# Attention stage: one-head loops, P times V in query halves, paired transposes and projections, diagonal blocks copied by GpSimd

## Time and profile before

| | us |
|---|---|
| median of 3 runs | 3308.22 (3308.05 to 3309.66) |
| the profiled execution | 3313.78 |
| its span, first to last instruction | 3312.2 |
| PE busy | 3196.9 (97%) |
| DVE busy | 2544.1 (77%) |
| ACT busy | 2007.7 (61%) |
| POOL busy | 1454.5 (44%) |

### The profile page before, as it was taken

The page is one execution under the profiler, slowest core; times in us unless marked ns, Lnnn a source line. Parts: engine busy times, 40 slices in busy tenths (PEclk is TensorE's granted clock), DMA queues, the critical chain, the costliest instruction groups (busy, mean ns, idle before and its releaser), DMA issues.

```text
span 3312.2 us, 54697 instructions
## 1 busy us (share of the span) xinstructions
PE 3196.9 (97%) x14467; PEld 1714.4 (52%) x14468; DVE 2544.1 (77%) x2917; ACT 2007.7 (61%) x3525; POOL 1454.5 (44%) x1795
## 2 busy tenths in 40 slices
PE   7799999998999999999999999999999999999998
PEld 3355444555555555555555555555555555555554
DVE  7612444234998989898988999898999899889995
ACT  4312320334676767676766777777777777777775
POOL 4677770013244444444444445544444444444443
PEclk9899999999999999999999999999999999999999
DMA  7613886665998989898988899999999999899997
GB/s 299 266 68 117 309 267 153 223 228 187 236 236 216 231 214 229 212 231 219 229 218 218 216 233 243 261 231 226 231 230 230 229 230 228 219 225 232 227 227 183
DMA packets 342733, 737.33 MB, mean 223 GB/s; under 512 B 129517, under 2 KB 177400, under 8 KB 342160
## 3 DMA queue, kind: packets, MB, share of 16 engines
q1 hardware_dynamic: 311056, 670.55, 76.9%
q0 software_dynamic: 31488, 64.51, 7.0%
HBM read 198.37 MB, written 159.51 MB: 108 GB/s over the span
## 4 chain that ended last, share of the span: by engine, by line
PE 70%; DVE 2%; issue 1%; SPq 1%; ACT 1%; DMA 0%; ACTq 0%; POOL 0%; DVEq 0%; POOLq 0%
PE at_ps L1043 27%; PE at_ps L1073 26%; PE at_ps L1056 9%; PE at_ps L1088 9%; DVE at_half_max L1164 1%; DVE at_blocks L1180 1%; SPq L914 1%; ACT at_prob L1124 0%; DMA at_v<-v_rows 0%; DMA at_moved<-at_blocks 0%; ACT at_scaled L1136 0%; DVE at_neg_max L1169 0%; ACT ahead_xe L1152 0%; SPq L905 0%; POOL at_acc L1003 0%
## 5 line engine op out<-in xcount | busy, mean ns | idle before, releaser
L1164 DVE TENSOR_REDUCE at_half_max<-at_ps 128x1 f32<-128x1024 f32 x1024 | 1206.6, 1219 | 250.9 <-PE at_ps L1043 249.0
L1124 ACT ACTIVATE at_prob<-at_ps,at_neg_max 128x1024 f32<-128x1024 f32 x1024 | 1145.3, 1118 | 333.7 <-DVE at_neg_max L1169 318.3
L1180 DVE STREAM_TRANSPOSE at_blocks<-at_prob 128x1536 f32<-128x1536 f32 x512 | 906.0, 1770 | 1.2 <-ACT at_prob L1124 1.2
L1043 PE MATMUL at_ps<-ahead_k_hl,ahead_q_hh 128*128 128x512 f32 x2048 | 854.4, 417 | 17.7 <-ACT at_prob L1124 10.8
L1003 POOL TENSOR_TENSOR at_acc<-at_acc,at_scaled 128x256 f32<-128x256 f32 x512 | 372.0, 727 | 1064.0 <-ACT at_scaled L1136 1064.0
L1043 PE MATMUL at_ps<-ahead_k_hl,ahead_q_ll 128*128 128x512 f32 x2048 | 810.2, 396 | 0.0
L1073 PE MATMUL at_ps<-at_moved,at_v 128*64 128x512 f32 x3072 | 726.8, 594 | 5.6 <-DMA at_moved<-at_blocks 4.3
L1136 ACT ACTIVATE at_scaled<-at_ps,at_inv 128x256 f32<-128x256 f32 x512 | 242.3, 473 | 354.1 <-PE at_ps L1088 340.0
L1056 PEld LDWEIGHTS at_ps<-keep_ident,at_prob 128*128 128x128 f32 x2048 | 216.1, 141 | 437.9 <-issue 425.5
L1043 PEld LDWEIGHTS at_ps<-ahead_k_hl,ahead_q_hh 128*128 128x128 f32 x2048 | 389.4, 190 | 88.2 <-ACT at_prob L1124 15.5
L1043 PEld LDWEIGHTS at_ps<-ahead_k_hl,ahead_q_ll 128*128 128x128 f32 x2048 | 390.4, 191 | 67.7
(11 more groups left out here) (112 smaller groups left out, 2596.1 us busy)
## 6 DMA issues: line engine op xcount, KB each, us to landing
at_moved<-at_blocks SPq DMA_DIRECT2D x2048, 192.0 KB
ahead_k_hl<-k_parts SPq DMA_DIRECT2D x64, 512.0 KB, 8.0
ahead_q_hh<-q_parts SPq DMA_DIRECT2D x128, 256.0 KB, 5.6
ahead_q_ll<-q_parts SPq DMA_DIRECT2D x128, 256.0 KB, 6.4
xbuf<-pr_zeros SPq DMA_DIRECT2D x32, 512.0 KB, 5.1
q_parts<-pr_part_hi SPq DMA_DIRECT2D x64, 256.0 KB
q_parts<-pr_part_lo SPq DMA_DIRECT2D x64, 256.0 KB
k_parts<-pr_part_hi SPq DMA_DIRECT2D x64, 256.0 KB, 2.2
```

What stands on the lines that cost most here:

```text
L1043: last = nc.tensor.matmul(ps[:, bank, :], q[:, g % 2, j * P:(j + 1) * P], k_hl[:, side, c * CH:(c + 1) * CH], start=first, stop=not first)
L1124: nc.scalar.activation(prob[:, i % 2, half * 1024:(half + 1) * 1024], ps[:, banks[0]:banks[1], :].rearrange("p b c -> p (b c)"), ACT.Exp, ...
L1164: nc.vector.tensor_reduce(half_max[:, i % 2, half:half + 1], ps[:, banks[0]:banks[1], :], AX.XY, ALU.max).then_inc(max_step, 1)
L1180: nc.vector.transpose(blocks[:, parity, :, j, :, :].rearrange("p c t k -> p t c k"), prob[:, (s["s"] - 1) % 2, 0:MOVED * P].rearrange("p ( ...
```

## The change

- The loop over heads has a body of one head. K is loaded twice per head, once for the first eight slots (side 0) and once for the last eight (side 1); W_O likewise.
- DVE turns 13 key tiles of 16, PE three. PE's transposes come in even slots, for the two tiles before, behind the scores, into banks of the early scores; one ACT copy takes both tiles out.
- P times V is done for each key tile in two query halves of 256 columns, so the two array halves hold two halves of the queries. The projection then contracts over 64 rows and gives all 128 queries of a tile; two tiles are projected in each odd slot, side by side on two halves of the rows.
- Of the 16 blocks of the exchange SP moves 12; the four on the diagonal, which stay on their partitions, are copied by POOL, two in each even slot (`diagonal`). P times V waits for `diag_done`.
- POOL gathers two rows in each of the even slots 0 to 6, and waits for them at the beginning of slots 2 to 8; scales and adds two in each of slots 8 to 14; and adds two scaled tiles in each odd slot.

```diff
-MOVED = 12
+MOVED = 13
 TURNED = NS - MOVED
 PV_LAG = 2 * GT
 OUT_LAG = 3 * GT + 1
-LAST = OUT_LAG + TILES
-PV_PLACES = ((12, 16), (0, 4), (4, 8), (8, 12))
+LAST = OUT_LAG + TILES - 1
+GQ = GT // 2
+PV_PLACES = ((13, 16), (0, 5), (5, 9), (9, 13))
 ACROSS = (0, 2, 1, 3)
 EARLY = ((0, 2), (4, 6))
 LATE = (2, 4)
-PV_BANK, TURN_BANK = 6, 7
+PV_BANK = 6
...
                     body(b, 0, s)
-                with eng.Fori(0, H // 2 - 1) as i:
-                    for u in (1, 2):
-                        for s in slots(b, (i, u)):
-                            body(b, (i, u), s)
+                with eng.Fori(1, H - 1) as h:
+                    for s in slots(b, h):
...
+            def next_k(b, h, side):
+                head = b * H + h
+                wait_apart(sp, late_scored, (head - 1) * TILES + (side + 1) * TILES // 2, sp_waits)
+                load_k(sp, scr, start, b, h, side)
...
             def load_wo(b, h, side):
-                wait_apart(sp, projected, (b * H + h - 1) * TILES + 1, sp_waits)
+                wait_apart(sp, projected, (b * H + h) * TILES - TILES // 2 * (1 - side), sp_waits)
...
-                for turn in range(QD):
+                for turn in range(1, QD):
                     for r, c in zip(ACROSS, ACROSS[turn:] + ACROSS[:turn]):
                         sp.dma_start(moved[c * 32:(c + 1) * 32, g % 2, r, :, :, :],
                                      blocks[r * 32:(r + 1) * 32, g % 2, c, :, :, :]
...
+            def head_loads(b, h, before, following):
                 next_q(b, h, 1)
+                next_k(b, h, 1)
                 if before is not None:
                     exchange(*before, GROUPS - 1)
                 next_q(b, h, 2)
                 load_v(b, h, 0)
                 exchange(b, h, 0)
-                load_wo(b, h, side)
+                load_wo(b, h, 0)
                 for place in range(1, GT):
                     load_v(b, h, place)
                 next_q(b, h, 3)
                 if following is not None:
-                    next_k(*following, 1 - side, 0)
+                    next_k(*following, 0)
                 exchange(b, h, 1)
                 if following is not None:
                     next_q(*following, 0)
-                    next_k(*following, 1 - side, 1)
                 exchange(b, h, 2)
+                load_wo(b, h, 1)
...
-                if k % (K // 2) == 0:
-                    wait_apart(pool, gathered[part], n * 64 + 64, pool_waits)
...
+                for k in (s["s"] % K, s["s"] % K + 1):
+                    if s["s"] < K:
+                        nc.gpsimd.indirect_dma_start(
+                            out=row(k), out_offset=None, in_=scr["ye"][:, :],
+                            in_offset=bass.IndirectOffsetOnAxis(ap=g_index[:, k:k + 1], axis=0),
+                            bounds_check=SLOTS, oob_is_err=True).then_inc(gathered[k // (K // 2)], 16)
+                    else:
+                        nc.gpsimd.tensor_scalar(row(k), row(k), g_gain[:, k:k + 1], None, ALU.mult
+                                                ).then_inc(g_scaled, 1)
+                        wait_apart(pool, g_scaled, n * K + k + 1, pool_waits)
+                        nc.gpsimd.tensor_tensor(into, into, row(k), ALU.add).then_inc(g_added, 1)
+                        wait_apart(pool, g_added, n * K + k + 1, pool_waits)
...
+            def diagonal(group, parity, r):
+
+                wait_apart(pool, blocks_done, GT * (group + 1), pool_waits)
+                wait_apart(pool, pv_done, GT * (group - 1), pool_waits)
+                for q in (r, r + 1):
+                    nc.gpsimd.tensor_copy(moved[q * 32:(q + 1) * 32, parity, q, :, :, :],
+                                          blocks[q * 32:(q + 1) * 32, parity, q, :, :, :]).then_inc(diag_done, 1)
+                    wait_apart(pool, diag_done, QD * group + q + 1, pool_waits)
...
+                if i % 2 == 0 and 0 < i <= K:
+                    part = (i - 1) // (K // 2)
+                    wait_apart(pool, gathered[part], s["head"] * 64 + 16 * (i - part * (K // 2)), pool_waits)
+                if s["diag"]:
+                    diagonal(*s["diag"])
...
             def score(s, half):
...
                     if j == 0:
                         pe.wait_ge(q_loaded[g % 2], 32 * (head * 2 + g // 2) + 32)
-                    if i == 0:
-                        pe.wait_ge(k_loaded[side], 32 * s["pair"] + 32)
+                    if i % (TILES // 2) == 0:
+                        pe.wait_ge(k_loaded[side], 16 * head + 16)
                     wait_pos(pe, early_exp, tile - 1)
+                    if i % 2:
+                        wait_pos(pe, copied, s["taken_all"])
+                    else:
+                        wait_pos(pe, scaled, s["projected"])
                     banks, done = EARLY[i % 2], early_scored
                 else:
                     wait_pos(pe, late_exp, tile)
...
             def transpose(s):
-                tile = s["tile"] - 2
-                pe.wait_ge(late_exp, tile + 1)
-                wait_pos(pe, copied, tile)
-                if s["out"]:
-                    wait_pos(pe, scaled, s["out"][0] * GT + s["out"][2])
-                for j in range(TURNED):
-                    t = MOVED + j
-                    last = nc.tensor.transpose(ps[:, TURN_BANK, j * P:(j + 1) * P],
-                                               prob[:, s["s"] % 2, t * P:(t + 1) * P], keep["ident"][:, :])
+
+                pe.wait_ge(late_exp, s["tile"])
+                pe.wait_ge(early_exp, s["tile"])
+                for a in range(2):
+                    for j in range(TURNED):
+                        t = MOVED + j
+                        last = nc.tensor.transpose(ps[:, EARLY[1][0] + a, j * P:(j + 1) * P],
+                                                   prob[:, a, t * P:(t + 1) * P], keep["ident"][:, :])
                 last.then_inc(turned, 1)
...
-                    pe.wait_ge(copied, GT * (group + 1))
+                    pe.wait_ge(copied, GT // 2 * (group + 1))
                     wait_pos(pe, oT_done, group)
                 else:
...
                 pe.wait_ge(v_loaded[place], 16 * (s["head"] + (1 if s["s"] >= PV_LAG else 0)))
                 for t in tiles:
-                    side = t % 2 * DH
-                    p_T = moved[:, parity, :, :, t, :] if t < MOVED else turned_sb[:, parity, t - MOVED, :, :, :]
-                    last = nc.tensor.matmul(ps[side:side + DH, PV_BANK, :], v[:, t, :], p_T,
-                                            start=(place == 0 and t < tiles[0] + 2),
-                                            stop=(place == GT - 1 and t >= tiles[-1] - 1))
+                    for half in range(2):
+                        side, queries = half * DH, slice(half * GQ, (half + 1) * GQ)
+                        p_T = (moved[:, parity, :, queries, t, :] if t < MOVED else
+                               turned_sb[:, parity, t - MOVED, :, queries, :])
+                        last = nc.tensor.matmul(ps[side:side + DH, PV_BANK, 0:GQ * P], v[:, t, :], p_T,
+                                                start=(place == 0 and t == tiles[0]),
...
             def project(s):
-                group, g, j, behind = s["out"]
...
-                for side in (0, DH):
-                    last = nc.tensor.matmul(ps[side:side + DH, TURN_BANK, 0:D],
-                                            oT[:, g % 2, j * P + side:j * P + side + DH], wo[:, s["out_side"], :],
-                                            start=True, stop=True)
-                last.then_inc(projected, 1)
+
+                for n, g, j, half, behind in s["out"]:
+                    if j == 0:
+                        pe.wait_ge(oT_done, s["pv_group"])
+                        pe.wait_ge(wo_loaded[g // 2], 16 * (s["head"] + (0 if behind else 1)))
+                    if half == 0:
+                        pe.wait_ge(early_exp, min(s["s"], TILES) + s["head"] * TILES)
+                        wait_pos(pe, scaled, n)
+                    rows, queries = slice(half * DH, (half + 1) * DH), slice(j % GQ * P, (j % GQ + 1) * P)
+                    nc.tensor.matmul(out_of(s, half), oT[rows, g % 2, queries], wo[rows, g // 2, :],
+                                     start=True, stop=True).then_inc(projected, 1)
...
             def body(b, h, s):
-                if s["late"]:
-                    transpose(s)
                 if s["scores"]:
                     score(s, 0)
                     score(s, 1)
-                if s["out"]:
-                    project(s)
+                project(s)
+                if s["taken"]:
+                    transpose(s)
                 if s["pv"]:
                     times_v(s)
...
             def take(s):
-                group, parity, j = s["turn"]
-                act.wait_ge(turned, s["tile"])
+                group, parity, j = s["taken"]
+                act.wait_ge(turned, s["taken_all"])
```

(56 more changed lines are left out.)

113 lines of the change are left out of this document (36 added, 77 removed).

## The result

The changed kernel takes 3646.07 us (median of 4 runs, 3632.79 to 3653.02) against 3308.14 us for the kernel before (4 runs, 3306.54 to 3309.66) beside it: a ratio of 1.1017, 95% interval 1.0983 to 1.105. The prediction said 3730, in a range of 3400 to 3900.

A forecast was written before the change was run, and what follows sets the result against it. GpSimd's ordered list was to become the period: 90.8 us a head against 77.3, 13.6 more for 31 heads, +422 on 3313.8 gives 3736, less the 5.6 by which the runs' median is lower: 3730 us; range 3400 to 3900.

The forecast's parts named there:

- Copy, 1.7 us: GpSimd's diagonal copies, 16 a head of 1664 elements per partition: 0.18 + 1.54 = 1.7 us each, bounds 0.41 and 4.8.
- Rivals 2 and 3: GpSimd's diagonal copies: cheap at 0.41 us, about 3110 us, chance 0.12; or far dearer at 4.8, about 5270, chance 0.04.
- Landing, 5.8 us: GpSimd's wait, in a head's first half, for two gathers to land before the next copies: 5.8 us per even-odd pair.
- Rival 1: Gathers land early in a head's first half: pairs of 9.4 us, head 80.4, about 3405 us; chance 0.13.
- Second half, 10.4 a pair: GpSimd's list per even-odd slot pair late in a head: copies 4.0, routed rows 4.14, additions 2.26, together 10.4 us.
- The sum: GpSimd's list per head: 4 x 12.0 + 4 x 10.4 + 1.2 = 90.8 us; 13.6 more for 31 heads, +422.
- The low end of the range: 3400 us for the whole kernel, said to be GpSimd copies of 1.6 us with gather landings of 3 us.
- PE, 4.3 to 4.4 us a slot: PE's attention work after the change: two slots cost 8.6 us plus up to 0.2, or 4.3 to 4.4 a slot.
- rival 2: Cheap GpSimd copies leave PE and VectorE as bound, winning 6.2 us on 32 heads: -198, about 3110 us; chance 0.12.
- VectorE, 4.4: VectorE's attention slot: 4.17 + 0.15 for the longer block transpose, plus sum and reciprocal, bringing 4.4 us.
- Jumps back: Loop jumps, 26 for 12: 0.7 us each where PE is the bound, nothing where PE waits anyway.
- Rival 4: Copies between 0.8 and 0.95 us, or GpSimd and PE gains meeting: within 7 us of 3308; chance 0.03.

The follow-up runs named there:

- e4: The change with each of GpSimd's 16 diagonal copies a head cut to 128 of 1664 elements per partition; ratio 0.9716 to the kernel before, 74.3 us a head.
- e5: The change with each of GpSimd's diagonal copies moving half its elements, 832 of 1664 per partition; ratio 0.9959 to the kernel before, 76.8 us a head.
- e7: The change with a group's four copies in slot 4g+6, gathers in fours after slots 2 and 6, awaited in 6 and 10; ratio 0.9995 to the kernel before.
- e1: The change with gathers in fours in slots 0 and 4, awaited in 4 and 8, and four copies together in slot 4g+8; ratio 1.0326 to the kernel before.
- e6: The change with SP moving groups 3 and 0's diagonal blocks, GpSimd copying only groups 1 and 2, gathers awaited in slots 8 and 10; 3240.21 us, ratio 0.9788.

## Why the prediction was right, and where its sizes were off

**The mechanism** was the one forecast. GpSimd's ordered list is the period; the landing stands behind copies that PE waits for. "GpSimd at 75% busy" was too high (62% of the span, 67% of the head above); the idle before its copies is put down to the gathers, PE is at 89% (75 to 80 forecast) with stops, VectorE is idle 14.7 us in the head above (20 forecast), DMA share is 0.74 (under 0.8 forecast). PE's 75 to 80% meant 70.4 us of work in 90.8; it was some 73.9 a head in e4 at a granted clock of 1.00, and 78.4 in the 87.6 of the head above at 0.94, which the forecast left out.

**Copy, 1.7 us**: measured 1.566, 8% less. Lengths of 128, 832 and 1664 took 286, 872 and 1566 ns: 0.83 ns per element plus 0.18 us. The rate of 0.93 taken from copies of 8 and 256 on 128 partitions was a little high, and the fixed part held. Rivals 2 and 3 fall with this. 16 copies x 0.13 = 2.1 us of the 2.8 by which the head was predicted too long.

**Landing, 5.8 us** from the second gather's issue: all gathers of the change landed in 2.8 to 11.5, median 5.8.

```profile
DMA to landing us min/median/max: 2.8/5.8/11.5
```

In the head above the first half's pairs took 11.8 on average where 12.0 (and 1.2 more for the index and jump) was said; less 3.7 for the copies, 2.2 for the gathers and 0.2 for the index that leaves about 5.7. Rival 1 fails with it: only the fastest gathers land in 3 us. The Trainium skill's fit ("DMA: Bandwidth & Descriptors", section "Anatomy of one DMA — SWDGE (gpsimd) path") would by estimate have had them all there in 2.3, and none was.

**Second half, 10.4 a pair**: 10.1.

**The sum**: head 90.8 predicted, 88.0 measured. Times 31 heads, +422 was said and some +335 came: 2.8 x 31 = 87 us, of which three quarters are the copy's rate. The term of the sum that was mis-sized is the copy, and with it nothing else of weight. The low end of the range was mis-summed: copies of 1.6 us with landings of 3 give 4 x 9.2 + 4 x 10.2 + 1.2 = 79 a head by the prediction's own terms, about 3360 us and not 3400.

**PE, 4.3 to 4.4 us a slot**: wrong, and hidden by GpSimd. With the copies shortened a slot is 4.63 to 4.64. Half of the four slots of e4 against my terms: transposes 0.69 (0.88 said), projection 0.67 (0.58), scores 4.13 (3.70), P times V 3.76 (3.44). That reads as if the scores had got slower, and they did not: the chain gives the overlap at a boundary to the piece before or behind. What counts is the time from the first start of a piece to the first start of the next, on PE's timeline, before and in e4:

```profile
2602.70 1.89 PE L1073 MATMUL at_ps<-at_moved,at_v 128*64 128x512 f32 x8
2604.52 0.66 PE L1056 MATMUL at_ps<-keep_ident,at_prob 128*128 128x128 f32 x4
```

```profile
2415.20 1.95 PE L1102 MATMUL at_ps<-at_moved,at_v 128*64 128x256 f32 x16
2417.08 0.50 PE L1070 MATMUL at_ps<-ahead_k_hl,ahead_q_hh 128*128 128x512 f32 x1
```

| per two slots, start to start | before us | e4 us | gain | gain said |
|---|---|---|---|---|
| transposes | 0.83 (8) | 0.76 (6) | 0.07 | 0.30 |
| projection | 0.96 | 0.63 | 0.33 | 0.58 |
| scores | 4.04 | 4.14 (0.04 of it a stop) | -0.10 | 0 |
| P times V | 3.64 | 3.76 | -0.12 | 0 |

I had cut pieces out of the earlier trace rows as if each were its own time; a piece taken away gives back less than its row says. P times V with twice as many products of half the width costs little more: 16 products of 256 columns take 1.88 us, 8 of 512 take 1.82. Had GpSimd not been in the way, "-198" would have been about -93 us, and rival 2 off by half.

**VectorE, 4.4**: its transposes of 1664 took 1.90 us (1.92 said); in e4 it is busy 769 of 800 us beside PE's 796. It was not shown to be a bound.

**Jumps back**: in e4 most heads, each with its jump, take 74.1 to 74.3 us in both batches, and four times the four slots above are 74.3; nothing is left for the jump (0.7 said).

**Rival 4's "everything cancels"** wanted copies of 0.8 to 0.95 us and a time within 7 us of the kernel before. e5 had 0.87 and came out 12 us below it: nearly so. e7 reached it with full copies, by another order of the same work. That was the step no case had: the sum was taken as given by the amounts, while 347 of the 439 us above e4's stage lay in where, and how often, the list waited. Taking the wait for the gathers away while copies stay behind them was not tried, because both then work on the same partitions without an order; what the landings alone cost is therefore shown only by moving them (e1, e7, e6).

## What to carry to other kernels

An engine that waits for each of its own operations has no slack of its own: cost its list as a sum, and put a wait for a transfer as far behind the issue, and as far ahead of what others need, as the list allows; that was worth 9% here with the same copies, gathers and additions. When a load can go to an engine or to the queues, share it by time: the queues while the engine waits for something, the engine while the queues are full. A piece of a chain of waits is not what its removal gives back; measure from the start of one piece to the start of the next.

## What the runs showed of the hardware

- GpSimd copies 32 partitions at 0.83 ns per element plus 0.18 us (286, 872, 1566 ns for 128, 832, 1664), hardly faster than 128 (256 elements on 128 partitions took 412 ns, where this line gives 392), and two in a row on different partitions take the sum, 3.19 us.
- PE's clock followed its stops: 0.91 in the half of a head with waits, 0.98 in the other, where 1 is 2.4 GHz. The product group behind a stop of 3.71 us ran at half its rate, 20 products in 4.54 us:

```profile
2413.43 4.54 PE L1098 MATMUL at_ps<-at_moved,at_v 128*64 128x256 f32 x20 [3.71 <-POOL at_moved L1004]
```

  against 2.31 in e4's row above. It was not on the chain here, GpSimd was.
- With the blocks back on the queues a DMA share of 1.03 went with 2.2 us more a head than e4's 0.88, one of 0.94 with 0.8 (there beside eight copies).
- Chips differ: on one of them the same kernel's stage began 138 us later (945.3 against 807.6) and then ran alike; on another the stages of e1 to e4 began at 936 to 948.
